# Three buffers instead of two for gathered embedding rows, and GpSimd's waits changed with them

## The chip, the cores and the metric

The kernel runs on one core of one Trainium2 chip. The metric is the device time of one execution in microseconds (us). Engines are named as the profile names them: PE is TensorE's matmul, PEld its weight load, DVE is VectorE, ACT is ScalarE, POOL is GpSimd, SP is SyncE.

## The reference

It is the forward pass of a recommendation model for 2048 samples. Each sample has 26 ids, one for each of 26 tables of 64-wide rows, and a dense vector of 256 values. Cut to what matters:

```
e = stack([tbl_f[ids[:, f]] for f in range(26)], axis=1)      # 2048 x 26 x 64
x = layer_norm(dense @ Wd.T, gd, bd)                          # 128 wide
y = layer_norm(einsum('bnd,ed->bne', e, Ws), gs, bs)          # 26 rows of 128
y = layer_norm(einsum('bne,pn->bep', y, Wsi), gsi, bsi)       # 26 mixed to 32
T = concatenate([x, y transposed], axis=1)                    # 33 x 128
Z = T @ T.transpose                                           # 33 x 33 a sample
z = layer_norm(lower_triangle(Z) @ Wl.T, gl, bl)[first 384]   # 528 -> 512
h = relu(concatenate([z, dense]) @ W_top1 + b_top1)
h = relu(h @ W_top2 + b_top2)
out = h @ W_top3                                              # one number a sample
```

## The kernel before, in words

The samples are cut into 16 tiles of 128 (`T = 16`), one sample in each partition. A tile t passes through stages that lie in up to four consecutive rounds u of one loop. Each engine has its own program, written out by hand in a fixed order, and in round u works on tile u (the gathered rows: transposed, their norms, normalized, shuffled), tile u-1 (mixing, projection, second normalization, gram matrices 0 to 2), tile u-2 (gram matrix 3, pair features, interaction, first layer) and tile u-3 (the other layers). Semaphores tie the engines together. Whatever waits on an engine holds up all that stands behind it in that engine's order.

What the change touches:

- GpSimd's program (lines 224 to 241). After two instructions that make an identity matrix, it does nothing but gather: 26 indirect DMAs for each tile, one for each feature (L239), 416 in all. Each fetches 128 rows of 64 floats by the ids in `idx`. They come in four batches of 8, 6, 6 and 6 features (`BATCHES`), and every batch counts on its own semaphore `gathered[t % 2][b]`. The rows go to `emb[t % 2]`, so tile t overwrites tile t-2.
- Ahead of a batch GpSimd waits for three things (lines 233 to 237). `nrm_ready` says that DVE has normalized the half of tile t-2 that the batch overwrites. `act_nrm`, ahead of batch 0, says that ACT has done its share of that normalization. `gram_done` says that PE has done gram matrix 0, 2, 3 and 3 of tile t-2 (`GATE = (1, 3, 4, 4)`) for the batches 0 to 3. Gram matrices 0, 1 and 2 of tile t-2 are made in round t-1, and gram matrix 3 is made near the start of round t.
- PE's round (lines 418 to 486) starts with `transposes(t0, 0)` (L296), which waits for batch 0 of the tile. Batches 1, 2 and 3 follow later in the same round. Between them stand the matrix products of the other tiles: mixing L314, projection L326, gram L338, interaction L381, the layers L399 and L407. ACT copies each transposed batch (L505), PE multiplies it (L305), DVE multiplies by `emb` and sums (L812, L816).
- Readers of `emb`: PE's transposes L296, DVE's L812 and L835, ACT's L518. After the normalization of a tile nothing reads its `emb` again. The gram matrices read `V`, which is made of the normalized rows two stages later (DVE L869).
- In the first rounds DVE and PE also prepare weights (`fold`, `prepare_wlt`), which no later round does.

Of the kernel before, what the change touches and what calls it, by code (L numbers as in the profile page):

```python
# [7 lines left out]
ALU = mybir.AluOpType  # L8
ACT = mybir.ActivationFunctionType
AXX = mybir.AxisListType.X  # L10

P = 128
NF, D = 26, 64
# [25 lines left out]
ACT_PIECES = 4  # L39

GATE = (1, 3, 4, 4)


def tri(i, j):
# [3 lines left out]
def after(engine, sem, value):  # L50

    if value > 0:
        engine.wait_ge(sem, value)
# [7 lines left out]
def tower(nc, a, out):  # L61
    T = a["ids"].shape[0] // P
    tables = [a[f"tbl_{f}"] for f in range(NF)]

    with ExitStack() as ctx:
        def sb(name, shape, dt=FP32):
            return ctx.enter_context(nc.sbuf_tensor(name, shape, dt))

        def bank(name, shape):
            return ctx.enter_context(nc.psum_tensor(name, shape, FP32))  # L70

        def sem(name):
            return ctx.enter_context(nc.semaphore(name))
# [17 lines left out]
        wmean = sb("wmean", [P, RC]); b1p = sb("b1p", [P, 4])  # L91

        idx = sb("idx", [P, T, NF], INT32)
        emb = [sb(f"emb{h}", [P, NF, D]) for h in range(2)]
        nrm = sb("nrm", [P, D, NP])
        byn = [sb(f"byn{h}", [P, NJ, D]) for h in range(2)]
        embt = sb("embt", [P, 4, P]); prod = [sb(f"prod{h}", [P, 8, D]) for h in range(2)]
# [26 lines left out]
        b_a, b_mix, b_y, b_z = bank("b_a", [P, 512]), bank("b_mix", [P, 512]), bank("b_y", [P, 2, 512]), bank("b_z", [P, 512])  # L124
# [11 lines left out]
            sem("wsq_zero"), sem("wsq_act"), sem("wsq_ready"), sem("gain_ready"), sem("wlt_ready"))  # L136
        idx_loaded = [sem(f"idx_loaded{h}") for h in range(2)]

        gathered = [[sem(f"gathered{h}{b}") for b in range(4)] for h in range(2)]
        emb_transposed, embt_copied, gw_done = sem("emb_transposed"), sem("embt_copied"), sem("gw_done")  # L140
        prod_done, varn_done, varm_done, stdn_done, rstdn_done, nrm_ready, act_nrm, byn_ready = (
            sem("prod_done"), sem("varn_done"), sem("varm_done"), sem("stdn_done"), sem("rstdn_done"), sem("nrm_ready"), sem("act_nrm"), sem("byn_ready"))
# [4 lines left out]
        gram_done, zs_copied, zb_ready, zt_done, zt_copied = (  # L147
            sem("gram_done"), sem("zs_copied"), sem("zb_ready"), sem("zt_done"), sem("zt_copied"))
# [19 lines left out]
        def features(b):  # L168
            return range(2 * BATCHES[b][0], 2 * BATCHES[b][-1] + 2)
# [53 lines left out]
        @block.gpsimd  # L223
        def _(pool):
            nc.gpsimd.memset(ident[:, :], 0.0).then_inc(ident_ready, 1)
            pool.wait_ge(ident_ready, 1)
            nc.gpsimd.affine_select(out=ident[:, :], in_=ident[:, :], compare_op=ALU.not_equal, fill=1.0, base=0,
                                    pattern=[[-1, P]], channel_multiplier=1).then_inc(ident_ready, 1)
            for t in range(T):
                if t < 2:  # L230
                    pool.wait_ge(idx_loaded[t], 16)
                for b in range(4):
                    after(pool, nrm_ready, 2 * (t - 2) + b // 2 + 1)
                    if b == 0:
                        after(pool, act_nrm, ACT_PIECES * (t - 1))

                    after(pool, gram_done, 4 * (t - 2) + GATE[b])
                    for f in features(b):
                        pool.indirect_dma_start(out=emb[t % 2][:, f, :], out_offset=None, in_=tables[f],  # L239
                                                in_offset=bass.IndirectOffsetOnAxis(ap=idx[:, t, f:f + 1], axis=0)  # L240
                                                ).then_inc(gathered[t % 2][b], 16)

        @block.tensor
        def _(pe):
# [45 lines left out]
                last.then_inc(wlt_mm, 1)  # L290

            def transposes(t, b):
                pe.wait_ge(gathered[t % 2][b], 16 * len(features(b)) * (t // 2 + 1))
                after(pe, prod_done, 4 * t + b)
                for n, c in enumerate(BATCHES[b]):
                    last = nc.tensor.transpose(b_a[:, n * P:(n + 1) * P], emb[t % 2][:, 2 * c:2 * c + 2, :].rearrange("p n d -> p (n d)"),  # L296
                                               ident[:, :])
                last.then_inc(emb_transposed, 1)

# [118 lines left out]
            for u in range(T + 3):  # L418
                t0, t1, t2, t3 = u, u - 1, u - 2, u - 3
                if real(t0):  # L420
                    transposes(t0, 0)
                    norms(t0, 0)
# [9 lines left out]
                if real(t0):  # L432
                    transposes(t0, 1)
# [25 lines left out]
                if real(t0):  # L459
                    transposes(t0, 2)  # L460
# [28 lines left out]
        def _(act):  # L489
# [23 lines left out]
            def normalize(t, lo, hi):  # L513

                act.wait_ge(rstdn_done, 2 * t + 1)
                after(act, byn_ready, 2 * t)
                for f in range(lo, hi):
                    last = nc.scalar.activation(nrm[:, :, f], emb[t % 2][:, f, :], ACT.Copy, scale=rstd_n[:, f:f + 1])  # L518
                last.then_inc(act_nrm, 1)

            def copy_mixed(t, c):
# [98 lines left out]
            for u in range(T + 3):  # L620
# [44 lines left out]
                if real(t0):  # L665
                    normalize(t0, 0, 4)
# [8 lines left out]
                if real(t0):  # L675
                    normalize(t0, 4, 7)
                    normalize(t0, 7, 10)
# [17 lines left out]
        def _(dve):  # L695
# [111 lines left out]
            def norms(t, b):  # L807
                n = len(features(b))
                f0 = features(b)[0]
                dve.wait_ge(gw_done, 4 * t + b + 1)  # L810
                after(dve, varn_done, 4 * t + b - 1)
                nc.vector.tensor_tensor(prod[b % 2][:, 0:n, :], b_a[:, 0:n * D].rearrange("p (n d) -> p n d", d=D),  # L812
                                        emb[t % 2][:, f0:f0 + n, :], ALU.mult).then_inc(prod_done, 1)
                dve.wait_ge(prod_done, 4 * t + b + 1)
                after(dve, varm_done, 2 * (t - 1) + b // 2 + 1)
                nc.vector.tensor_reduce(var_n[:, f0:f0 + n], prod[b % 2][:, 0:n, :], AXX, ALU.add).then_inc(varn_done, 1)  # L816
# [7 lines left out]
            def normalize(t, k):  # L824

                f0, n = HALVES[k][0], len(HALVES[k])
                dve.wait_ge(stdn_done, 2 * t + k + 1)
                after(dve, nrm_ready, 2 * (t - 1) + k + 1)
                if k == 0:
                    after(dve, act_nrm, ACT_PIECES * t)  # L830
                nc.vector.reciprocal(rstd_n[:, f0:f0 + n], std_n[:, f0:f0 + n]).then_inc(rstdn_done, 1)  # L831
                dve.wait_ge(rstdn_done, 2 * t + k + 1)
                after(dve, byn_ready, 2 * t)
                for f in range(max(f0, ACT_FEATURES), f0 + n, 2):
                    last = nc.vector.tensor_tensor(nrm[:, :, f:f + 2].rearrange("p d n -> p n d"), emb[t % 2][:, f:f + 2, :],  # L835
                                                   rstd_n[:, f:f + 2].unsqueeze(2).broadcast_to([P, 2, D]), ALU.mult)
                last.then_inc(nrm_ready, 1)

# [59 lines left out]
            for u in range(T + 2):  # L898
                t0, t1, t2 = u, u - 1, u - 2
                if real(t0):  # L900
                    norms(t0, 0)
# [11 lines left out]
                if real(t0):  # L913
                    norms(t0, 1)
# [15 lines left out]
                if real(t0):  # L930
                    norms(t0, 2)
                    normalize(t0, 0)
# [12 lines left out]
                if real(t0):  # L945
                    normalize(t0, 1)
                    shuffle(t0)
# [26 lines left out]
```

## Time and profile before

| | us |
|---|---|
| median of 3 runs (607.56 to 610.67) | 608.56 |
| profiled execution, its own time | 609.85 |
| its span, first to last instruction | 608.0 |
| mean granted TensorE clock, share of full | 0.989 |

| stretch of the span (us) | PE busy | DVE busy | ACT busy | POOL busy |
|---|---|---|---|---|
| 116 to 149 | 30.60 | 29.22 | 20.84 | 25.08 |
| 149 to 182 | 30.71 | 28.75 | 20.37 | 24.92 |
| 281 to 314 | 30.58 | 29.05 | 20.74 | 25.08 |
| 479 to 512 | 30.96 | 29.48 | 21.23 | 24.75 |
| 545 to 608 | 52.14 | 35.23 | 31.35 | 0.47 |

The second table gives the busy time in stretches of 33 us, about one round each, and in the last 63 us, in which there is nothing left to gather. Busy time of POOL holds only the recorded pieces of its instructions, without the gaps between them. A row of the timeline reads: start in us, duration in us, engine, line, operation, output<-inputs, count, and in brackets how long the engine had been idle and what ended that.

### The profile page before, as it was taken

The page shows a single profiled execution, that of the slowest core. Times are in us where ns is not written, and L with a number is a line of the kernel's source. Part 1 is how long each engine was busy: PE and PEld are TensorE (multiplying, and loading weights), DVE is VectorE, ACT ScalarE, POOL GpSimd, SP SyncE. Part 2 cuts the span into 40 slices and gives each one's busy share as a digit, 9 for nine tenths or more (in the row PEclk, how much of TensorE's full clock was granted, in tenths as well). Part 3 has the DMA queues.
Part 4 walks back from the last instruction along what each step waited for, and adds up shares of the span by engine and source line. Part 5 has one row for each costly group of instructions (what it writes and reads, how often), then busy time and mean ns, then how long its engine had stood idle before and what let it go on. Part 6 is the DMA issues. An engine that isn't in the chain of part 4 may idle for free.

```text
span 608.0 us, 17689 instructions
## 1 busy us (share of the span) xinstructions
PE 523.0 (86%) x6955; PEld 389.3 (64%) x6955; DVE 499.1 (82%) x977; ACT 338.4 (56%) x922; POOL 401.0 (66%) x422
## 2 busy tenths in 40 slices
PE   2466858999998989999999989898998999998996
PEld 1354636585867667675758576667667585857575
DVE  5985599998889796888889898979888898988750
ACT  4003364666566565656566666657574666666642
POOL 6777456777777777777777777777777777760000
PEclk9999997999999998999999999999999999999999
DMA  7311011111111111111111111111111111110000
GB/s 171 109 25 38 17 26 24 36 28 28 38 28 36 28 38 27 36 26 37 27 36 30 27 37 28 37 28 37 27 37 28 37 28 27 29 28 3 1 3 1
DMA packets 22611, 20.23 MB, mean 33 GB/s; under 512 B 12016, under 2 KB 14720, under 8 KB 22528
## 3 DMA queue, kind: packets, MB, share of 16 engines
q0 software_dynamic: 13312, 13.66, 11.7%
q1 hardware_dynamic: 8400, 4.33, 2.7%
q8 instruction: 55, 0.90, 0.6%
q10 hardware_dynamic: 816, 1.11, 0.6%
q14 instruction: 28, 0.23, 0.1%
HBM read 19.07 MB, written 0.01 MB: 31 GB/s over the span
## 4 chain that ended last, share of the span: by engine, by line
PE 40%; POOL 25%; issue 14%; DVE 10%; DMA 5%; ACT 5%; SPq 0%; POOLq 0%; ACTq 0%; DVEq 0%
POOL emb L239 25%; PE b_l L381 7%; PE b_y L326 6%; PE b_mix L314 6%; DMA emb<-in_tbl,idx 4%; PE b_a L305 4%; PE b_z L338 4%; PE b_l L407 3%; PE b_a L296 2%; PE b_l L399 2%; ACT nrm L518 1%; DVE V L869 1%; ACT embt L505 1%; PE b_l L369 1%; PE b_l L414 1%
## 5 line engine op out<-in xcount | busy, mean ns | idle before, releaser
L239 POOL DMA_INDIRECT emb<-in_tbl,idx x416 | 400.3, 962 | 143.7 <-issue 122.3
L851 DVE TENSOR_TENSOR yb<-b_y,bias_y 128x1024 f32<-128x1024 f32 x64 | 78.3, 1223 | 38.7 <-PE b_y L326 36.8
L505 ACT ACTIVATE embt<-b_a 128x512 f32<-128x512 f32 (+1 forms) x64 | 32.7, 512 | 125.9 <-PE b_a L296 125.9
L869 DVE TENSOR_TENSOR V<-yb,rstd_y 128x256 f32<-128x256 f32 x256 | 91.9, 421 | 2.2
L326 PE MATMUL b_y<-mixed,projw 64*128 64x512 f32 x256 | 73.5, 650 | 13.9 <-ACT mixed L524 13.5
L858 DVE TENSOR_REDUCE var_y<-sq 128x32 f32<-128x1024 f32 x64 | 77.1, 1205 | 2.4 <-ACT sq L529 2.4
L305 PE MATMUL b_a<-gram_w,embt 128*128 128x128 f32 x416 | 65.3, 299 | 15.1 <-ACT embt L505 15.1
L314 PEld LDWEIGHTS b_mix<-mix,byn 128*128 128x128 f32 x512 | 65.5, 200 | 16.1 <-issue 13.4
L305 PEld LDWEIGHTS b_a<-gram_w,embt 128*128 128x128 f32 x416 | 56.7, 205 | 29.2 <-ACT embt L505 19.6
L314 PE MATMUL b_mix<-mix,byn 128*128 128x128 f32 x512 | 73.3, 288 | 1.9 <-DVE byn L846 1.7
L524 ACT ACTIVATE mixed<-b_mix 128x512 f32<-128x512 f32 x64 | 38.3, 598 | 58.6 <-PE b_mix L314 58.1
L529 ACT ACTIVATE sq<-yb 128x1024 f32<-128x1024 f32 x64 | 67.2, 1051 | 2.6 <-DVE yb L851 1.3
L518 ACT ACTIVATE nrm<-emb,rstd_n 128x64 f32<-128x64 f32 x192 | 53.5, 395 | 12.2 <-DVE rstd_n L831 12.2
L846 DVE STREAM_TRANSPOSE byn<-nrm 128x1024 f32<-128x1024 f32 x32 | 59.4, 1930 | 0.6
L381 PE MATMUL b_l<-wlt,zt 128*128 128x512 f32 x128 | 59.2, 605 | 0.0
L338 PE MATMUL b_z<-V 128*32 128x34 f32 x4096 | 54.8, 201 | 3.0 <-DVE V L869 1.6
L338 PEld LDWEIGHTS b_z<-V 128*32 128x32 f32 x4096 | 46.4, 111 | 13.6 <-issue 6.4
L399 PE MATMUL b_l<-z_t,w 128*128 128x128 f32 x384 | 53.3, 275 | 0.0
L296 PE MATMUL b_a<-ident,emb 128*128 128x128 f32 x208 | 36.7, 293 | 18.3 <-DMA emb<-in_tbl,idx 14.0
L399 PEld LDWEIGHTS b_l<-z_t,w 128*128 128x128 f32 x384 | 48.0, 192 | 0.0
L540 ACT ACTIVATE zs<-b_z 128x272 f32<-128x272 f32 x64 | 40.9, 638 | 10.4 <-PE b_z L338 10.0
L296 PEld LDWEIGHTS b_a<-ident,emb 128*128 128x128 f32 x208 | 26.1, 150 | 30.3 <-DMA emb<-in_tbl,idx 16.6
(134 smaller groups left out, 722.0 us busy)
## 6 DMA issues: line engine op xcount, KB each, us to landing
emb<-in_tbl,idx POOLq DMA_INDIRECT x416, 2.4
dense<-in_r_dense_t SPq DMA_DIRECT2D x16, 128.0 KB, 2.2
V<-in_L_rec_Wl ACTq DMA_DIRECT2D x1, 1056.0 KB, 5.3
w<-in_W_top SPq DMA_DIRECT2D x2, 512.0 KB
w<-in_W_top SPq DMA_DIRECT2D x1, 768.0 KB
out_y<-y_sb SPq DMA_DIRECT2D x16, 0.5 KB
idx<-in_ids SPq DMA_DIRECT2D x1, 195.0 KB, 5.1
wd<-in_L_rec_Wd SPq DMA_DIRECT2D x1, 128.0 KB
```

Of the source, the lines that this page charges most:

```text
L239: pool.indirect_dma_start(out=emb[t % 2][:, f, :], out_offset=None, in_=tables[f], in_offset=bass.IndirectOffsetOnAxis(ap=idx[:, t, f:f + ...
L296: last = nc.tensor.transpose(b_a[:, n * P:(n + 1) * P], emb[t % 2][:, 2 * c:2 * c + 2, :].rearrange("p n d -> p (n d)"), ident[:, :])
L305: last = nc.tensor.matmul(b_a[:, n * P:(n + 1) * P], embt[:, n, :], gram_w[:, :], start=True, stop=True)
L314: last = nc.tensor.matmul(b_mix[:, m * P:(m + 1) * P], byn[t % 2][:, j:j + 2, :].rearrange("p j d -> p (j d)"), mix[:, :], start=True, sto ...
L326: last = nc.tensor.matmul(b_y[:, j2, :], projw[r, :], mixed[c % 2][r, :], start=True, stop=True, tile_position=(64 * j2, 0))
L338: last = nc.tensor.matmul(b_z[32 * q:32 * q + 32, GRAM * j:GRAM * (j + 1)], v[:, 0:NP], v, start=True, stop=True)
L381: nc.tensor.matmul(b_l1[:, :], zt[:, c, :], wlt[:, c, :], start=(c == 0), stop=False)
L399: last = nc.tensor.matmul(dst, w1[:, c, m * P:(m + 1) * P], rhs, start=(n == 0), stop=(n == 4))
L529: nc.scalar.activation(sq[:, :, :, :], yb[c % 2][:, :, :, :], ACT.Square, scale=NP ** -0.5).then_inc(y_squared, 1)
L851: nc.vector.tensor_tensor(yb[c % 2][:, :, :, :].rearrange("e h s p -> e (h s) p"), b_y[:, :, :].rearrange("e h (s p) -> e (h s) p", p=NP), ...
L858: nc.vector.tensor_reduce(var_y[c % 2][:, :], sq[:, :, :, :].rearrange("e h s p -> e (h s) p"), AXX, ALU.add).then_inc(vary_done, 1)
L869: last = nc.vector.tensor_tensor(V[t % 2][:, j2, c, m:m + 2, :, 0:NP].rearrange("e m q p -> e (m q) p"), yb[c % 2][:, j2, 4 * m:4 * m + 8, :],
```

## The change

`emb` gets a third buffer (26 x 64 floats in each of 128 partitions), and `gathered` a third set of semaphores. Everything that indexed them by t % 2 does so by t % 3, and what each wait counts follows. GpSimd's waits for `nrm_ready` and `act_nrm` now look at tile t-3, and the wait for `gram_done` is gone.

```diff
-GATE = (1, 3, 4, 4)
+NE = 3
...
-        emb = [sb(f"emb{h}", [P, NF, D]) for h in range(2)]
+        emb = [sb(f"emb{h}", [P, NF, D]) for h in range(NE)]
...
-        gathered = [[sem(f"gathered{h}{b}") for b in range(4)] for h in range(2)]
+        gathered = [[sem(f"gathered{h}{b}") for b in range(4)] for h in range(NE)]
...
                 for b in range(4):
-                    after(pool, nrm_ready, 2 * (t - 2) + b // 2 + 1)
+                    after(pool, nrm_ready, 2 * (t - NE) + b // 2 + 1)
                     if b == 0:
-                        after(pool, act_nrm, ACT_PIECES * (t - 1))
-
-                    after(pool, gram_done, 4 * (t - 2) + GATE[b])
+                        after(pool, act_nrm, ACT_PIECES * (t - NE + 1))
+
                     for f in features(b):
-                        pool.indirect_dma_start(out=emb[t % 2][:, f, :], ...
+                        pool.indirect_dma_start(out=emb[t % NE][:, f, :], ...
...
-                                                ).then_inc(gathered[t % 2][b], 16)
+                                                ).then_inc(gathered[t % NE][b], 16)
...
-                pe.wait_ge(gathered[t % 2][b], 16 * len(features(b)) * (t // 2 + 1))
+                pe.wait_ge(gathered[t % NE][b], 16 * len(features(b)) * (t // NE + 1))
```

The four reads of `emb[t % 2]` (L296, L518, L812, L835) become reads of `emb[t % NE]`.

## Rows read from the trace of the kernel before

**Rows 1.** The page, part 1: busy us (share of the span) xinstructions of PE.

```profile
PE 523.0 (86%) x6955; PEld 389.3 (64%) x6955; DVE 499.1 (82%) x977; ACT 338.4 (56%) x922; POOL 401.0 (66%) x422
```

**Rows 2.** Waits: engine line <- waited for: us in total, times, longest us.

```profile
POOL emb L239 <- PE b_z L338: 18.4, 13, 11.6
PE b_a L296 <- DMA emb<-in_tbl,idx: 14.0, 13, 6.8
```

**Rows 3.** The line L239: duration ns min/median/max, first and last start; then landing.

```profile
L239 POOL DMA_INDIRECT emb<-in_tbl,idx x416: 938/944/1642, 3.3 to 544.4; - x139
...
DMA to landing us min/median/max: 2.3/2.4/3.9
```

**Rows 4.** Timeline of POOL: last gather of tile 1, then firsts of batches.

```profile
68.87 0.94 POOL L239 DMA_INDIRECT emb<-in_tbl,idx  x1 [0.30 <-issue]
81.39 0.94 POOL L239 DMA_INDIRECT emb<-in_tbl,idx  x1 [11.58 <-PE b_z L338]
...
93.32 0.95 POOL L239 DMA_INDIRECT emb<-in_tbl,idx  x1 [1.99 <-PE b_z L338]
...
101.58 0.94 POOL L239 DMA_INDIRECT emb<-in_tbl,idx  x1 [0.83 <-PE b_z L338]
...
116.65 0.94 POOL L239 DMA_INDIRECT emb<-in_tbl,idx  x1 [0.30 <-issue]
...
512.93 0.95 POOL L239 DMA_INDIRECT emb<-in_tbl,idx  x1 [0.30 <-issue]
```

**Rows 5.** Timeline of PE, line L296: starts of rounds; 103.51, 201.63, 269.21 are batch 1.

```profile
62.11 1.06 PE L296 MATMUL b_a<-ident,emb 128*128 128x128 f32 x4
...
94.02 1.06 PE L296 MATMUL b_a<-ident,emb 128*128 128x128 f32 x4
...
103.51 0.55 PE L296 MATMUL b_a<-ident,emb 128*128 128x128 f32 x3 [0.58 <-DMA emb<-in_tbl,idx]
...
127.88 0.55 PE L296 MATMUL b_a<-ident,emb 128*128 128x128 f32 x3 [0.30 <-DMA emb<-in_tbl,idx]
...
193.54 0.66 PE L296 MATMUL b_a<-ident,emb 128*128 128x128 f32 x4 [0.36 <-DMA emb<-in_tbl,idx]
...
201.63 0.49 PE L296 MATMUL b_a<-ident,emb 128*128 128x128 f32 x3
...
227.53 0.55 PE L296 MATMUL b_a<-ident,emb 128*128 128x128 f32 x3 [1.55 <-DMA emb<-in_tbl,idx]
...
261.00 0.49 PE L296 MATMUL b_a<-ident,emb 128*128 128x128 f32 x3
...
269.21 0.49 PE L296 MATMUL b_a<-ident,emb 128*128 128x128 f32 x3
...
459.23 0.55 PE L296 MATMUL b_a<-ident,emb 128*128 128x128 f32 x3 [1.34 <-DMA emb<-in_tbl,idx]
...
491.64 0.60 PE L296 MATMUL b_a<-ident,emb 128*128 128x128 f32 x4
...
524.25 0.55 PE L296 MATMUL b_a<-ident,emb 128*128 128x128 f32 x3 [0.42 <-DMA emb<-in_tbl,idx]
```

**Rows 6.** Stretches: PE, PEld, DVE, ACT, POOL busy (x), PEclk, DMA share, GB/s.

```profile
70.20:81.30 11.10, 9.24 (x110) 6.46 (x109) 7.90 (x13) 5.23 (x10) 0.00 (x0) 1.00 0.02 4
89.90:100.10 10.20, 7.83 (x125) 6.69 (x122) 9.99 (x22) 4.79 (x16) 6.38 (x8) 0.50 0.11 21
...
229.90:233.30 3.40, 3.40 (x76) 3.10 (x76) 1.38 (x2) 0.97 (x2) 1.92 (x3) 0.51 0.15 28
```

**Rows 7.** Stretch of one round: the same columns.

```profile
182.00:215.00 33.00, 30.52 (x431) 22.78 (x430) 28.99 (x56) 20.67 (x56) 24.90 (x26) 1.00 0.15 32
```

**Rows 8.** Line L869 after the last gather, then between 94 and 545 us.

```profile
L869 DVE TENSOR_TENSOR V<-yb,rstd_y x24: 418/420/427, 548.9 to 583.5; 128x256 f32<-128x256 f32 x24
...
L869 DVE TENSOR_TENSOR V<-yb,rstd_y x220: 410/419/478, 97.9 to 544.2; 128x256 f32<-128x256 f32 x110
```

**Rows 9.** Timeline of DVE: the first projection's result in round 5.

```profile
198.97 1.22 DVE L851 TENSOR_TENSOR yb<-b_y,bias_y 128x1024 f32<-128x1024 f32 x1 [1.23 <-PE b_y L326]
```

More of the change, by code:

```diff
@@ L232, in _ @@
                 for b in range(4):
-                    after(pool, nrm_ready, 2 * (t - 2) + b // 2 + 1)
+                    after(pool, nrm_ready, 2 * (t - NE) + b // 2 + 1)
                     if b == 0:
-                        after(pool, act_nrm, ACT_PIECES * (t - 1))
-                    after(pool, gram_done, 4 * (t - 2) + GATE[b])
+                        after(pool, act_nrm, ACT_PIECES * (t - NE + 1))
                     for f in features(b):
-                        pool.indirect_dma_start(out=emb[t % 2][:, f, :], out_offset=None, in_=tables[f],
+                        pool.indirect_dma_start(out=emb[t % NE][:, f, :], out_offset=None, in_=tables[f],
                                                 in_offset=bass.IndirectOffsetOnAxis(ap=idx[:, t, f:f + 1], axis=0)
-                                                ).then_inc(gathered[t % 2][b], 16)
+                                                ).then_inc(gathered[t % NE][b], 16)
         @block.tensor
@@ L292, in transposes @@
             def transposes(t, b):
-                pe.wait_ge(gathered[t % 2][b], 16 * len(features(b)) * (t // 2 + 1))
+                pe.wait_ge(gathered[t % NE][b], 16 * len(features(b)) * (t // NE + 1))
                 after(pe, prod_done, 4 * t + b)
                 for n, c in enumerate(BATCHES[b]):
-                    last = nc.tensor.transpose(b_a[:, n * P:(n + 1) * P], emb[t % 2][:, 2 * c:2 * c + 2, :].rearrange("p n d -> p (n d)"),
+                    last = nc.tensor.transpose(b_a[:, n * P:(n + 1) * P], emb[t % NE][:, 2 * c:2 * c + 2, :].rearrange("p n d -> p (n d)"),
                                                ident[:, :])
@@ L517, in normalize @@
                 for f in range(lo, hi):
-                    last = nc.scalar.activation(nrm[:, :, f], emb[t % 2][:, f, :], ACT.Copy, scale=rstd_n[:, f:f + 1])
+                    last = nc.scalar.activation(nrm[:, :, f], emb[t % NE][:, f, :], ACT.Copy, scale=rstd_n[:, f:f + 1])
                 last.then_inc(act_nrm, 1)
@@ L812, in norms @@
                 nc.vector.tensor_tensor(prod[b % 2][:, 0:n, :], b_a[:, 0:n * D].rearrange("p (n d) -> p n d", d=D),
-                                        emb[t % 2][:, f0:f0 + n, :], ALU.mult).then_inc(prod_done, 1)
+                                        emb[t % NE][:, f0:f0 + n, :], ALU.mult).then_inc(prod_done, 1)
                 dve.wait_ge(prod_done, 4 * t + b + 1)
@@ L834, in normalize @@
                 for f in range(max(f0, ACT_FEATURES), f0 + n, 2):
-                    last = nc.vector.tensor_tensor(nrm[:, :, f:f + 2].rearrange("p d n -> p n d"), emb[t % 2][:, f:f + 2, :],
+                    last = nc.vector.tensor_tensor(nrm[:, :, f:f + 2].rearrange("p d n -> p n d"), emb[t % NE][:, f:f + 2, :],
                                                    rstd_n[:, f:f + 2].unsqueeze(2).broadcast_to([P, 2, D]), ALU.mult)
```

## The prediction

> **What bounds the kernel now.** I read the busy shares first, then who waits for whom, then the timelines of POOL and of PE's line L296, and last some stretches of the span. The busy shares single nobody out: PE 86%, DVE 82% [rows 1]. POOL's 66% misleads, and its own rows say why. A gather's record takes 944 ns (median), but 0.30 us of idle stands ahead of each, put down to issue [rows 3, 4]. The pace of POOL is therefore 1.24 us for each of 26 gathers. From the first gather of tile 3 (116.65) to that of tile 15 (512.93) are 396.28 us in 12 tiles, 33.02 us each [rows 4]. Its only sizable wait in there is one in tile 6: POOL's 13 waits on gram matrices sum to 18.4 us, of which 11.58, 1.99 and 0.83 lie in tile 2 and nine are the ordinary 0.30, which leaves 1.3, or 1.0 above the ordinary [rows 2, 4]. Free of waits it needs 32.9 us for a tile, and from tile 3 on it is hardly ever idle.
>
> PE's rounds have the same pace, since each begins with the transposes of a tile just gathered: from 127.88 to 524.25 are 396.37 us in 12 rounds, 33.03 each [rows 5]. In all but two of those rounds PE arrives a little before the rows do: at 193.54 it had waited 0.36 us, at 227.53 1.55 us, at 459.23 1.34 us, at 524.25 0.42 us [rows 5]. In total PE waited 14.0 us for gathers in 13 places; the longest, 6.8, is the very first tile's [rows 2], which no buffer can help. So 7.2 us in 12 places remain. PE's round without those waits is short of POOL's by little. I name this: two engines almost balanced, POOL slower by 0.5 us a tile.
>
> POOL has been held back early. After the last gather of tile 1 (68.87) it sat idle 11.58 us until gram matrix 0 of tile 0, then 1.99 and 0.83 us more for later gram matrices [rows 4]. Taking the ordinary 0.30 off each, that is 11.28 + 1.69 + 0.53 = 13.5 us in which the slower of two balanced engines did nothing. Its buffer was long free.
>
> **The change, part by part.**
>
> *The wait on gram matrices goes.* It costs POOL 18.4 us in 13 places [rows 2]; nine of these are the ordinary 0.30 us, which stay. Of the other four, 13.5 us lie in tile 2 and 1.0 in tile 6. Tile 2's gathers now start at 68.87 + 1.24 = 70.1, not 81.39, and tile 3's at 116.65 - 13.5 = 103.1.
>
> *What does POOL wait for next?* For the normalization of tile t-3. That work ends a whole round before the one on t-2 for which POOL waits now. Tile 3's gathers at 103.1 need tile 0 normalized, and PE is by then in round 2 (from 94.02), whose DVE order has tile 1 done. From then on POOL's tile t is about one round ahead of where PE needs it, while the buffer allows nearly two. I take this wait at nothing. If POOL ran faster than I think it would block, harmlessly, since then the rows are there.
>
> *Does PE ever wait again?* Batch 0 of a tile is complete 7 x 1.25 + 0.94 + 2.4 = 12.1 us after its first gather starts (eight gathers, and 2.4 us to landing [rows 3]). Tile 2: 70.1 + 12.1 = 82.2 against PE's need at 94.02, a lead of 11.8 us. The lead shrinks by what PE's round is shorter, 0.5 us a tile: 11.8 - 13 x 0.5 = 5.3 us left at tile 15. The wait doesn't come back within 16 tiles. The gain is therefore set by PE's own pace, not by POOL's 13.5 us.
>
> *PE's own pace.* Intervals between round starts, less the wait that ended them: 227.53 to 261.00 is 33.47, in which the clock fell (below); 459.23 to 491.64 is 32.41, no wait; 491.64 to 524.25 is 32.61 - 0.42 = 32.19 [rows 5]. So does 193.54 to 227.53, 33.99 - 1.55 = 32.44. I take 32.4. As a sum: the 7.2 us of waits go. One, 0.58 us, is batch 1 of tile 2 at 103.51; the other eleven are batch 0's [rows 2, 5]. Round 2 itself starts no sooner than 94.02: there PE came straight from other work, with no wait recorded [rows 5].
>
> *The clock.* From 229.90 to 233.30 PE ran at a granted clock of 0.51, the 1.2 GHz level, just after its 1.55 us wait [rows 5, 6]. That round took 33.47 us against 32.4, so the dip cost 1.0 us. The wait of 1.34 us at 459.23 brought none. I expect the dip to go with its wait and count 1.0, bounds 0 and 1.0. The other dip, 89.90 to 100.10 at 0.50 [rows 6], comes where PE has little to do in round 1 with DVE busy 9.99 of 10.20 us; gathers have no part in it, so I leave it.
>
> *What takes the freed time.* PE is in a ring with DVE and ACT. DVE waited 1.23 us for the first projection of round 4's tile at 198.97 [rows 9]. It is busy 28.99 us of 33 [rows 7], so it has margin, and a round 0.4 us shorter doesn't use it up. But when DVE came late, as at 261.00, batch 1 followed batch 0 after 8.21 us, not the 8.09 after 193.54 [rows 5]. If that 0.12 us is paid in 12 rounds it returns 1.4 us at most; at least it returns nothing. I take 0.7.
>
> *Third buffer, semaphores, index arithmetic.* No instruction is added on any engine; a wait already satisfied cost POOL nothing beyond its 0.30 [rows 4]. Other tiles of memory move to other addresses. No row can price that; I take nothing, and bound it by half a round's shortening either way, 0.2 us x 14 = +-2.8.
>
> *POOL beside DVE.* From 70.20 to 81.30 POOL now works where it was idle, with DVE 7.90 us busy [rows 6]. Later, POOL's phase against DVE slides by 0.5 us a tile where the gates used to hold it. What does a gather beside it cost DVE? The line L869, with both inputs in SBUF, has a median of 420 ns after the last gather and 419 ns with POOL gathering; its longest is 478 [rows 8]. So 0 us is the near bound. The far one is 0.058 us on each of 16 such instructions, 0.93 us a tile, which the 1.23 us of DVE's wait would still hide. I take 0.
>
> The Trainium skill (page "SBUF — State Buffer", section "Who interferes with whom") speaks against this: a DVE instruction with two SBUF inputs contends with a GpSimd instruction that reads SBUF, and whichever comes second blocks fully. If it held for gathers, more overlap would mean more blocking of DVE. The trace doesn't agree for L869 as shown: 419 ns beside POOL's work, 420 without.
>
> **Sum, against the profiled execution's own 609.85 us (span 608.0 and 1.85 around it):** 609.85 - 7.2 - 1.0 + 0.7 = 602.4. That execution lay 1.3 us above the median of the runs, 608.56, so the time to compare with a median is 601.1; I say 601.
>
> **The rivals.**
>
> *B: the waits come back half from the ring.* For it: DVE, 29 us busy and with waits on ACT it can't shed, is near the bound too; PE's rounds net of waits already scatter from 32.19 to 32.44. Against: round 13's 32.41 without any wait. Half of 7.2 and no clock gain: 609.85 - 3.6 - 1.3 = 605.0.
>
> *C: all of POOL's lost time comes back.* If PE's own round were 32.0 or less, the kernel would follow POOL, which ends 13.5 + 1.0 us sooner: 608.56 - 14.5 = 594. For it: round 1, less filled, took 31.9 (62.11 to 94.02) [rows 5]. Against: no full round is below 32.19.
>
> *D: no change.* The 0.3 to 0.4 us waits are a symptom, PE being early because of slack elsewhere in a round of 33.0 that another engine sets. Then 608.5. Against: the rounds with long waits are longer by about those waits.
>
> *S: slower, GpSimd blocks DVE.* The gates hold POOL in step with the round; free, its gathers slide over the four L869 groups and the two halves of L835. If each of these six groups were held up by half a gather (0.47 us), DVE would lose 2.8 us a tile, 1.6 beyond its 1.23 of margin. Over 13 tiles that is 20.8, less the gain of 7.5: 608.6 + 13.3 = 622. It decides for slower once DVE loses 1.23 + 0.6 = 1.8 us a tile, about two gathers' worth. Against: POOL gathers in 24.90 of 33 us already, and nothing of it shows in L869 [rows 7, 8]. The Trainium skill ("SBUF — State Buffer", "Who interferes with whom") has a rule by which this would be the outcome; the trace so far doesn't bear it out.
>
> *That the change doesn't do what it says* would need POOL to be still idle after tile 1. No wait I can find would hold it; this goes with D.
>
> **How the numbers follow.** Forecast 0.55, B 0.20, C 0.07, D with all near no change 0.12, S 0.06. The forecast's own range is 598 to 604, from the bounds of clock, return and addresses. Leaving out most of C, half of D and S, the range is 597 to 606.5. What this kernel's measurement can tell from no change is about 0.5%, 3.0 us, so faster means below 605.5: all of the forecast and C and most of B, 0.80. Same (605.5 to 611.6) 0.14, slower 0.06.
>
> **What would show it.** In the profile after: POOL's gap at 81.39 gone, tile 2's first gather at 70.1, the last gather near 530 and not 544.4. PE's waits for gathers down from 14.0 in 13 places to one, about 6.8 us. Round starts 32.3 to 32.5 us apart, round 2 still at 94, round 15 at about 516. L869 still at 419 to 421 ns. I would be wrong if the rounds stayed at 33.0 with PE's waits moved to ACT's or DVE's results (D or B), or if DVE's durations grew (S).

## The result, and the profile after

The changed kernel took 600.75 us (median of 4 executions, 598.70 to 604.25); the kernel before took 608.06 us (median of 4). The ratio is 0.9871, 95% interval 0.9834 to 0.9907. The profiled execution took 602.28 us, with a span of 600.2 us. The forecast was 601.

Lines after the change are one lower than before: L296 is now L295, L338 is L337, L869 is L868.

The page's part 1 of the changed kernel, which answers to [rows 1]. Busy times are nearly the old ones; the span shrank around them:

```profile
PE 520.4 (87%) x6955; PEld 388.9 (65%) x6955; DVE 498.3 (83%) x977; ACT 338.5 (56%) x922; POOL 402.3 (67%) x422
```

The waits of the changed kernel (us in total, times, longest), which answer to [rows 2]. POOL's wait on gram matrices is absent, and of PE's 13 waits for gathers the first tile's is left:

```profile
POOL emb L238 <- issue: 125.5, 412, 0.3
...
PE b_a L295 <- DMA emb<-in_tbl,idx: 6.7, 1, 6.7
```

The page's part 4, the chain of work that ended last, as shares of the span by engine. First the kernel before, then the changed one, in whose chain POOL no longer stands:

```profile
PE 40%; POOL 25%; issue 14%; DVE 10%; DMA 5%; ACT 5%; SPq 0%; POOLq 0%; ACTq 0%; DVEq 0%
...
PE 54%; DVE 24%; issue 11%; ACT 9%; DMA 1%; SPq 0%; DVEq 0%; ACTq 0%
```

POOL's timeline, which answers to [rows 4]: the last gather of tile 1, then the first gathers of tiles 2, 3 and 15, then the last of all. No gap is left ahead of tile 2:

```profile
70.03 0.94 POOL L238 DMA_INDIRECT emb<-in_tbl,idx  x1 [0.30 <-issue]
71.28 0.95 POOL L238 DMA_INDIRECT emb<-in_tbl,idx  x1 [0.30 <-issue]
...
104.13 0.95 POOL L238 DMA_INDIRECT emb<-in_tbl,idx  x1 [0.30 <-issue]
...
499.18 0.94 POOL L238 DMA_INDIRECT emb<-in_tbl,idx  x1 [0.30 <-issue]
...
530.89 0.94 POOL L238 DMA_INDIRECT emb<-in_tbl,idx  x1 [0.30 <-issue]
```

PE's timeline of L295, which answers to [rows 5]: starts of the rounds 2, 3, 14 and 15, with batch 1 of round 2 at 102.78. None of them has a wait on a gather:

```profile
93.92 0.64 PE L295 MATMUL b_a<-ident,emb 128*128 128x128 f32 x2
...
102.78 0.49 PE L295 MATMUL b_a<-ident,emb 128*128 128x128 f32 x3
...
127.48 0.49 PE L295 MATMUL b_a<-ident,emb 128*128 128x128 f32 x3
...
482.47 0.60 PE L295 MATMUL b_a<-ident,emb 128*128 128x128 f32 x4
...
514.92 0.49 PE L295 MATMUL b_a<-ident,emb 128*128 128x128 f32 x3
```

Twelve rounds take 514.92 - 127.48 = 387.4 us, 32.29 each, against 396.4 and 33.03. In the same rounds of both kernels, stretches (length; busy us of PE, PEld, DVE, ACT, POOL; PEclk, DMA share, GB/s) show two halves of the difference. First the kernel before:

```profile
127.90:524.20 396.30, 365.85 (x5160) 273.44 (x5160) 345.72 (x649) 246.16 (x660) 299.35 (x312) 1.00 0.16 32
```

and the changed one, with its second stretch of low clock:

```profile
127.50:514.90 387.40, 361.54 (x5162) 271.24 (x5161) 345.08 (x649) 246.19 (x660) 294.16 (x307) 1.00 0.14 32
...
588.60:592.00 3.40, 3.40 (x19) 3.40 (x18) 0.00 (x0) 0.10 (x1) 0.00 (x0) 0.51 0.00 0
```

PE's idle time (the length less its busy time) fell from 30.45 to 25.86 us, 4.6 less. Its busy time fell by 4.3. After round 15's start the changed kernel needed 600.2 - 514.9 = 85.3 us against 608.0 - 524.2 = 83.8 before, since it ran at half clock from 588.6 to 592.0.

### The profile page after: what moved, and what is told of

It is laid out like the page before. It is cut to its first block, busy times and chain, and to the rows that moved or that the text cites. A ratio compares the mean times of both kernels' runs of the same rounds, so it can differ in the third digit from the quotient of the medians.

```text
span 600.2 us, 17646 instructions
## 1 busy us (share of the span) xinstructions
PE 520.4 (87%) x6955; PEld 388.9 (65%) x6955; DVE 498.3 (83%) x977; ACT 338.5 (56%) x922; POOL 402.3 (67%) x422
## 4 chain that ended last, share of the span: by engine, by line
PE 54%; DVE 24%; issue 11%; ACT 9%; DMA 1%; SPq 0%; DVEq 0%; ACTq 0%
PE b_y L325 8%; PE b_l L398 7%; PE b_l L380 7%; PE b_mix L313 7%; DVE V L868 5%; PE b_a L304 5%; PE b_z L337 5%; PE b_l L406 5%; DVE var_y L857 3%; ACT nrm L517 3%; DVE byn L845 2%; PE b_a L295 2%; DVE prod L811 2%; DVE nrm L834 2%; PE b_l L368 2%
## 5 line engine op out<-in xcount | busy, mean ns | idle before, releaser
L504 ACT ACTIVATE embt<-b_a 128x512 f32<-128x512 f32 (+1 forms) x64 | 32.8, 513 | 116.7 <-PE b_a L295 116.7
L868 DVE TENSOR_TENSOR V<-yb,rstd_y 128x256 f32<-128x256 f32 x256 | 91.8, 421 | 2.2
L313 PE MATMUL b_mix<-mix,byn 128*128 128x128 f32 x512 | 72.5, 286 | 2.1 <-DVE byn L845 1.7
L337 PE MATMUL b_z<-V 128*32 128x34 f32 x4096 | 53.9, 201 | 4.0 <-DVE V L868 2.7
L337 PEld LDWEIGHTS b_z<-V 128*32 128x32 f32 x4096 | 45.7, 110 | 14.7 <-issue 6.2
L295 PE MATMUL b_a<-ident,emb 128*128 128x128 f32 x208 | 36.2, 291 | 11.1 <-DMA emb<-in_tbl,idx 6.7
L380 PEld LDWEIGHTS b_l<-wlt,zt 128*128 128x128 f32 x128 | 23.0, 189 | 34.5 <-issue 34.5
```

Source lines behind the costliest of these rows:

```text
L313: last = nc.tensor.matmul(b_mix[:, m * P:(m + 1) * P], byn[t % 2][:, j:j + 2, :].rearrange("p j d -> p (j d)"), mix[:, :], start=True, sto ...
L337: last = nc.tensor.matmul(b_z[32 * q:32 * q + 32, GRAM * j:GRAM * (j + 1)], v[:, 0:NP], v, start=True, stop=True)
L380: nc.tensor.matmul(b_l1[:, :], zt[:, c, :], wlt[:, c, :], start=(c == 0), stop=False)
L868: last = nc.vector.tensor_tensor(V[t % 2][:, j2, c, m:m + 2, :, 0:NP].rearrange("e m q p -> e (m q) p"), yb[c % 2][:, j2, 4 * m:4 * m + 8, :],
```

## The experiments

All times are medians, with the ratio to the kernel before on the same chip. The last three columns are the first gather of tile 2, the first gather of tile 15 and the start of round 15, from each kernel's timeline.

| kernel | us | ratio (95%) | tile 2 | tile 15 | round 15 |
|---|---|---|---|---|---|
| before | 608.06 | 1 | 81.4 | 512.9 | 524.2 |
| changed | 600.75 | 0.9871 (0.9834 to 0.9907) | 71.3 | 499.2 | 514.9 |
| changed, again | 601.18 | 0.9836 (0.9801 to 0.9870) | 71.2 | 499.2 | 514.9 |
| two buffers, no gates | 601.47 | 0.9858 (0.9827 to 0.9889) | 71.1 | 499.2 | 514.9 |
| three buffers, gates kept | 608.63 | 0.9970 (0.9949 to 0.9990) | 81.4 | 511.7 | 522.9 |
| gates on tile 2 only | 609.23 | 0.9991 (0.9971 to 1.0011) | 80.7 | 510.3 | 522.4 |
| gates on all but tile 2 | 606.79 | 0.9946 (0.9921 to 0.9971) | 71.1 | 508.4 | 519.6 |
| batch 0 of tile 2 waits | 605.97 | 0.9915 (0.9881 to 0.9950) | 80.6 | 508.7 | 520.1 |
| tile 2 waits for gram 2 | 619.36 | 1.0123 (1.0070 to 1.0175) | 93.0 | 520.4 | 531.9 |
| tile 2 waits for a square | 600.70 | 0.9828 (0.9784 to 0.9873) | 72.5 | 501.8 | 513.0 |
| gathers for three tiles | 598.17 | 0.9776 (0.9730 to 0.9822) | 70.1 | none | 513.0 |
| memsets in their place | 599.39 (one execution) | 0.984 (one pair) | 70.2 | none | 513.5 |
| another order on ACT | 600.52 | 0.9838 (0.9808 to 0.9868) | 71.5 | 499.6 | 513.9 |

### Which half of the change carries the gain

The kernel before, without its gram waits and with nothing else changed:

```diff
-                    after(pool, gram_done, 4 * (t - 2) + GATE[b])
```

> Two buffers as before, the waits on gram matrices taken away, the waits on normalization of tile t-2 kept. My theory: the gram waits alone held POOL, the buffer did not. Tile 3's gathers, at about 104 us, need tile 1 normalized, which ends with round 1 at 94; tile 15's, at 499, need tile 13, done at about 482. So POOL starts tile 2 at about 71 us, never waits, and the time is that of the changed kernel, 600.8 within 1.5. Rival: the third buffer carries the gain, POOL is caught by the normalization of tile t-2 and the time stays above 605.

It took 601.47 us, and its timeline is the changed kernel's. POOL, first gather of tile 15:

```profile
499.22 0.94 POOL L237 DMA_INDIRECT emb<-in_tbl,idx  x1 [0.31 <-issue]
```

The changed kernel with the gram waits put back:

```diff
+                    after(pool, gram_done, 4 * (t - 2) + GATE[b])
```

> Three buffers and the waits on normalization of tile t-3, but the gram waits of before put back. My theory: nothing changes from before, POOL's gap of 11.6 us ahead of tile 2 is there, round 15 starts at 524, 608 within 1.5. Rival (the buffer carries the gain): 601 to 604.

It took 608.63 us, a ratio of 0.997 (0.9949 to 0.9990): with the gates in place the third buffer gives 0.1 to 0.5%, against 1.3% for the change. So the gates held POOL; the third buffer didn't bring the gain, and the kernel with two shows that it wasn't needed for it.

### What a delay of POOL costs

The same wait, for some tiles only:

```diff
+                    if t == 2:
+                        after(pool, gram_done, 4 * (t - 2) + GATE[b])
```

> The changed kernel with the gram waits put back for tile 2 alone. My theory: POOL needs 32.9 us a tile against PE's 32.3 a round, so what it loses at tile 2 it never makes up. Tile 3 starts at 116.6, tile 15 has its first batch at 116.6 + 12 x 32.92 + 12.1 = 523.8, so round 15 starts at 523.8 against 524.25 before and 514.8 after: 607 to 608. Rival: the gates in every later round are what costs, and one delay early is absorbed; then 601 to 602.

The other kernel has `if t != 2` there.

> The changed kernel with the gram waits put back for all tiles except tile 2. My theory: gram matrix 0 of tile 1 comes about 18.8 us into round 2, so tile 3's gathers start at about 113.3 instead of 104.1; POOL's lead is cut to some 2 us and gone two or three tiles later. Tile 15's first batch lands at 113.3 + 0.8 + 12 x 32.92 + 12.1 = 521.2, round 15 starts there, 6.4 us later than after: 606 to 607. The rival (only the delay at tile 2 costs): 601.

Both theories held, one of them not in its number. One delay in tile 2 costs all of the gain. It took 609.23 us, above the 607 to 608 expected, although round 15 started at 522.4 and not at 523.8: its profile has 6.8 us at half clock between 594 and 602, behind round 15. The gates in the later tiles cost most of the gain too (606.79): the wait ahead of tile 3 is 8.66 us once tile 2 has none, against 9.78 ahead of tile 2 in the other kernel. POOL's timeline of the kernel with gates on all but tile 2, first gather of tile 3:

```profile
112.38 0.94 POOL L241 DMA_INDIRECT emb<-in_tbl,idx  x1 [8.66 <-PE b_z L340]
```

The costs of the two don't add: with all gates kept POOL reaches tile 3 at 116.7 and finds its gram matrix made, while here it gets there sooner and waits until 112.4. This profile differs from the changed kernel's in one more thing. Two products of a projection take 0.70 us at 68.4, and 1.23 us in the changed kernel at about the same time (first row, second row):

```profile
68.41 0.70 PE L328 MATMUL b_y<-mixed,projw 64*128 64x512 f32 x2 [0.78 <-ACT mixed L526]
...
68.55 1.23 PE L325 MATMUL b_y<-mixed,projw 64*128 64x512 f32 x2 [0.78 <-ACT mixed L523]
```

So I take PE to have come to its full clock some 5 us earlier here, though the granted clock reads 1.00 in both. Round 2 started at 92.0, not 93.9; round 15's 519.6 thus answers to 521.5 on equal terms, and 521.2 was expected.

Three kernels delay batch 0 of tile 2 alone, by waiting for gram matrix 0, gram matrix 2, or ACT's first square:

```diff
+                    if t == 2 and b == 0:
+                        after(pool, gram_done, 1)      # or gram_done, 3; or y_squared, 1
```

> The changed kernel, in which batch 0 of tile 2 alone waits for gram matrix 0 of tile 0, at about 81.4 us, 10.1 us later than POOL would start it; no other gram wait. My theory: 10.1 less the lead of 3.5 is paid, +6.6: 607.4 within 1.5. Rival (only the whole set of gates costs, one is absorbed in the 11.8 us of lead at tile 2): 601.

> The changed kernel, in which batch 0 of tile 2 alone waits for gram matrix 2 of tile 0. That comes at about 93.3 us, 22 us after POOL would have started tile 2, about twice the delay of the kernel before. My theory: of a delay d at tile 2, all but POOL's final lead is paid; the lead at tile 15 in the profile after is 514.8 - (499.2 + 12.1) = 3.5 us. So +18.5 us: 619 within 2, with rounds 32.9 us apart and PE waiting for gathers in every round. Rival: later slack absorbs half of it, 611 or less.

> The changed kernel, in which batch 0 of tile 2 alone waits for the first square of ACT (L528), which ends at about 75.3 us: POOL starts tile 2 some 4.3 us late, 0.8 more than the lead of 3.5 that it has left at tile 15. My theory: the delay is absorbed but for 0.8 us at the very end, 601 to 602, and PE waits for gathers in the last two or three rounds alone. Rival (every us that POOL loses is paid): +4.3, 605.

Measured: 605.97, 619.36 and 600.70 us. In the first, tile 2 began 9.4 us later than in the changed kernel and round 15 5.2 us later. The last was delayed much less than meant: POOL waited 2.68 us, its tile 2 began only 1.2 us later, and PE waited for a gather in rounds 14 and 15 only. PE's timeline of it, those two rounds:

```profile
480.30 0.55 PE L297 MATMUL b_a<-ident,emb 128*128 128x128 f32 x3 [0.36 <-DMA emb<-in_tbl,idx]
...
513.00 0.55 PE L297 MATMUL b_a<-ident,emb 128*128 128x128 f32 x3 [0.33 <-DMA emb<-in_tbl,idx]
```

That is a lead used up to the last, but not by the delay alone. PE also began round 2 at 91.9 and not 93.9 (the earlier clock again), and POOL began tile 15 2.6 us later, 1.2 of it lost between tiles 3 and 15. So this run doesn't test whether a delay of 4.3 us is absorbed. The table shows the lead of the others: in the seven profiles with delays or gates, round 15 starts 11.2 to 12.1 us after POOL began tile 15. In five of them PE waited for that gather, and there it is 11.2 to 11.4, the time a batch takes to be gathered. Without a delay it is 15.7, and 14.3 with the other order on ACT.

POOL, first gather of tile 2 with the longest delay:

```profile
92.99 0.94 POOL L240 DMA_INDIRECT emb<-in_tbl,idx  x1 [23.21 <-PE b_z L339]
```

It came 21.7 us later than in the changed kernel and round 15 came 17.0 us later. The lead took 4.4 and the few tenths that POOL's pace varies.

### Does gathering slow the other engines

POOL's loop ends after three tiles, so the later tiles are computed on the rows left in the buffers:

```diff
-            for t in range(T):
+            for t in range(NE):
...
-                pe.wait_ge(gathered[t % NE][b], 16 * len(features(b)) * (t // NE + 1))
+                pe.wait_ge(gathered[t % NE][b], 16 * len(features(b)))
```

> POOL gathers tiles 0 to 2 only and is idle from about 104 us on; the later tiles are computed on the rows left in the three buffers. My theory: in the changed kernel PE no longer waits for gathers and POOL's work costs DVE nothing, so rounds stay at 32.27 us, the same lines of DVE keep their durations (L868 419 to 421 ns), and the time is 600.8 within 1.5. Rival (POOL's gathers block DVE): rounds under 32 us and 596 or less.

It took 598.17 us, between the two theories and outside what mine allowed. Not DVE changed but PE. First the groups of lines (busy us, mean ns | idle before) in rounds 3 to 14 of the changed kernel:

```profile
L337 PE MATMUL b_z<-V 128*32 128x34 f32 x3072 | 40.1, 199 | 1.1 <-DVE V L868 1.1
...
L868 DVE TENSOR_TENSOR V<-yb,rstd_y 128x256 f32<-128x256 f32 x192 | 68.9, 421 | 1.6
```

and of the kernel that gathers for three tiles:

```profile
L337 PE MATMUL b_z<-V 128*32 128x34 f32 x3072 | 36.9, 199 | 2.1 <-DVE V L868 1.8
...
L868 DVE TENSOR_TENSOR V<-yb,rstd_y 128x256 f32<-128x256 f32 x192 | 68.8, 420 | 1.6
```

DVE's busy time in these rounds is 345.08 us with the gathers and 344.95 without. The products of the gram matrices are as long one by one (199 ns) but lie further apart while POOL gathers. On PE's timeline of the changed kernel, 64 of them, once not stretched and once stretched:

```profile
156.11 0.77 PE L337 MATMUL b_z<-V 128*32 128x34 f32 x64
...
188.41 0.95 PE L337 MATMUL b_z<-V 128*32 128x34 f32 x64
```

Of 46 such runs of 64 that its timeline lists whole in rounds 3 to 14, 23 take 0.77 us and 23 take 0.79 to 0.97; with nothing gathered all take 0.77. PE's busy time in these rounds fell by 2.8 us (361.54 to 358.79), but 1.3 of it came back as waits, so that they are 1.5 us shorter.

One more kernel asked what stretches them. It is the one with gathers for three tiles, and GpSimd then writes zeros instead:

```diff
+            for t in range(NE, T):
+                pool.wait_ge(nrm_ready, 2 * (t - NE) + 2)
+                for f in range(NF):
+                    after(pool, junk_done, NF * (t - NE) + f)
+                    nc.gpsimd.memset(junk[:, :], 0.0).then_inc(junk_done, 1)
```

> As the run that gathers for three tiles only, but for the later tiles GpSimd makes 26 memsets of 128x1024 each on a tile that nobody reads, one after the other, and no DMA. It asks what stretches the 64 products of a gram matrix (L337) on PE from 0.77 us to 0.9 or 1.0 in every second round while POOL gathers (with POOL idle all are 0.77). If GpSimd's instructions do it, the stretched ones are back and rounds are 32.27 us or more; if the gathers' transfers or descriptors do it, all stay at 0.77 and rounds at 32.15. I expect the second.

It took 599.39 us in a single execution, with rounds of 32.2 us. PE's group of the same line, in rounds 3 to 14:

```profile
L344 PE MATMUL b_z<-V 128*32 128x34 f32 x3072 | 36.9, 199 | 2.6 <-DVE V L875 2.6
```

With GpSimd 952 ns busy per memset and nothing gathered, none is stretched. So it comes with the gathers, not with GpSimd's being busy. Which part of a gather does it (GpSimd's work of issuing it, its transfers, or something beside them) was not tried.

### Shortening PE's round

The changed kernel with another order: DVE's `recip_o(t2)` ahead of `normalize(t0, 0)`, and on ACT

```diff
-                    normalize(t0, 0, 4)
-                if real(t2):
-                    scale_o(t2)
-                if real(t0):
-                    copy_embt(t0, 3)
-                if real(t2):
-                    copy_z(t2)
+                if real(t2):
+                    scale_o(t2)
+                if real(t0):
+                    copy_embt(t0, 3)
+                if real(t2):
+                    copy_z(t2)
+                if real(t0):
+                    normalize(t0, 0, 4)
```

> The changed kernel with another order around batch 3: DVE makes the reciprocal for tile t-2 before it normalizes tile t, and ACT scales z, copies the transposed batch 3 and z's transpose before its first four normalizations. In the profile after, PE waits there for ACT 0.7 us a round, in the order of the chain. My theory: PE's round of 32.27 us sets the pace, so it falls to 31.6 to 31.9; POOL at 32.92 a tile then has its 3.5 us of lead used up after some six rounds and becomes the bound again, so no more than 3.5 us come back: 597.3, with PE waiting for gathers in the last six rounds or more. Rivals: the whole 0.5 us in 13 rounds comes back, 594; or DVE or ACT sets the round and nothing comes, 600.8 (the last square of y is 0.5 us later in this order).

It took 600.52 us: nothing. The wait it aimed at went, but the rounds 3 to 14 still took 387.4 us. PE's groups in them, and the stretch as a whole:

```profile
L304 PE MATMUL b_a<-gram_w,embt 128*128 128x128 f32 x312 | 45.1, 283 | 11.3 <-ACT embt L504 11.3
...
L337 PE MATMUL b_z<-V 128*32 128x34 f32 x3072 | 41.2, 199 | 2.5 <-DVE V L868 0.8
...
126.50:513.90 387.40, 364.15 (x5163) 272.26 (x5162) 345.43 (x650) 245.43 (x660) 294.10 (x307) 1.00 0.14 32
```

In the changed kernel PE's wait for z's scaling was 8.3 us in these rounds, and that for `embt` 8.2. Here the first is gone and the second 11.3. The gram products grew by 1.1. So PE arrives earlier and waits elsewhere. Its busy time rose by 2.6 us while its idle time fell by as much, so busy time of PE isn't a fixed amount of work either. My claim that PE's own program sets the round is too narrow. I take it to be the ring of PE, ACT and DVE, which is argued from these waits and not shown: which link of it holds at 32.29 us I did not settle, and that POOL would bind again at a shorter round stays untested.

## Why the prediction was right, step by step

*What bounds.* Right. POOL needed (499.18 - 104.13) / 12 = 32.92 us a tile, as forecast, and is now ahead of PE. Putting any sizable delay back makes it the bound again.

*Which wait mattered.* Right, and sharper than written: removing the gram wait alone does all (601.47 us). I gave the wait for tile t-3 no cost; the same holds for the wait for tile t-2. The third buffer with its new addresses, taken at nothing with a bound of 2.8 us, cost nothing: round 15 starts at 514.93 with two buffers and no gates, and at 514.92 with three.

*The lead.* The mechanism was right, one term mis-sized. I added 0.94 us for the last gather's own record and 2.4 to landing, 12.1 in all. The rows say 11.3 (512.93 to 524.25 in [rows 4, 5]), since landing counts from a gather's start. POOL's tile 2 also began at 71.3 and not 70.1, as its first gather started 0.5 us later and some in the start-up took longer. The final lead was 514.9 - 499.2 - 11.3 = 4.4 us, forecast 5.3. It never decided the sum.

*The waits of 7.2 us.* All went, PE's 14.0 us became 6.7. But other idle time of PE came back in rounds 3 to 14: there 6.4 us of waits went and idle fell by 4.6, so 1.8 returned: 1.1 is PE waiting for DVE's V, and 0.8 is PE waiting longer for ACT's scaled z. PE's group of that line before and after, in these rounds:

```profile
L390 PE MATMUL b_l<-ident,z 128*128 128x128 f32 x36 | 6.6, 291 | 7.5 <-ACT z L596 7.5
...
L389 PE MATMUL b_l<-ident,z 128*128 128x128 f32 x36 | 6.6, 291 | 8.3 <-ACT z L595 8.3
```

I had taken 0.7 for it with a bound of 1.4, too low. Against this, PE's busy time fell by 4.3 us, which I had not forecast beyond the clock. Part of it must be the vanished dip. By their groups, mixing fell by 0.9 us, the gram products by 1.0 and the transposes of gathered rows by 0.6; what shortened them was not tried. PE's rounds came out at 32.29, not 32.4.

*The clock.* The dip at 229.9 [rows 6] is gone, as forecast. But a like one fell at 588.6 and cost 1.5 us where nothing hides it. Forecast to take 1.0 us off the time, the clock in sum added 0.5 in the profiled execution. That the dip belonged to the wait of 1.55 us stays unproven, and more speaks against it: waits of 1.49 and 1.26 us (two kernels with batch 0 of tile 2 delayed) and of 1.05 and 1.02 us (gates on all but tile 2) had none, one of 1.02 us (gates on tile 2 only) was followed by one at 458.4, and the one at 588.6 came after the last gather. I also overlooked that POOL's only long wait after tile 2, 1.23 us at 233.66 for a gram matrix, ended right behind the dip of 229.90 to 233.30. By its place it looks like the same event: the gates let a slow stretch of PE hold up POOL too.

*The sum.* By the spans: 9.3 us were gained by round 15's start and 1.5 lost after it, 7.8 together, against 7.5 forecast. That it came so close is in part luck. Rounds 3 to 14 gave 8.9 us, where my terms gave 6.7 (6.4 of waits and 1.0 of clock, less 0.7), and the half clock at 588.6, which I hadn't forecast, took 1.5 back.

*The rivals.* B (half of it returns) had something of the truth in the 1.8 us. C was out: it wanted PE's own round at 32.0 or less, and it is 32.15 us even with nothing gathered. D fell with the delays. S had the right question and the wrong engine: gathers do slow another engine, but it is PE's gram products, by 3.2 us over twelve rounds, while L868 is at 419 ns median and 458 at the longest. The page "SBUF — State Buffer" of the Trainium skill, section "Who interferes with whom", would have DVE blocked when both its inputs lie in SBUF and GpSimd reads there; for these gathers no run here shows it. The same section also says, as an inference, that `tensor_tensor` (which L868 is) takes only the shared read interface while writing descriptors needs the write interface. I had passed over that; the 419 ns agree with it.

## What to carry to other kernels

When two engines run at nearly the same pace, as here, the time that the slower one is held up early is paid at the end, less the lead that it has left; read each engine's own pace from its first and last instruction of a kind before trusting its busy share. A wait that orders a producer behind something it doesn't need can cost more than a missing buffer: try taking away the wait first, as two buffers do here what three do. Count what the next-slowest engine allows, not what the wait was long: 13.5 us of idle on POOL were worth 7 to 8.

## What the runs showed of the hardware

Indirect DMAs on GpSimd stretch dense runs of small products on PE: 64 products of 128x34 take 0.77 us with none in flight and up to 0.97 us with them in the changed kernel, and memsets on GpSimd don't do it. Two things differ between the profiles of these kernels: in two of them the products at 68 us already run at their short duration (0.70 us for two, against 1.23), and round 2 starts 2 us earlier; and stretches of 3.4 us at half clock fall in different places, or not at all behind round 15. They may well be what makes executions of one kernel differ (598.70 to 604.25 us), but that isn't shown: the only two profiles of one kernel, the changed one, are alike (round 15 at 514.92 and 514.88).
